# Two attention layers on one core: keys projected from split operands and copied straight into the key stacks, and a new order inside every attention step

## What is computed

```python
x       (16, 100, 256)      # tokens, normalised ahead of each part
ctx     (16, 361, 256)      # context rows, the same for both layers
q = split_heads(queries @ Wq + bq)
k = split_heads(keys @ Wk + bk)
v = split_heads(values @ Wv + bv)
scores = einsum('bhqd,bhkd->bhqk', q, k) / sqrt(HD)
scores = where(mask, -1e15, scores)          # layer 0 only
attn = softmax(scores, axis=-1)
ctx = einsum('bhqk,bhkd->bhqd', attn, v)
out = ctx @ Wo + bo
x = x + tanh(g) * out
```

## Time and profile before

| | us |
|---|---|
| median of three runs | 870.8 (870.23 to 872.3) |
| span of the profiled execution | 871.8 |
| what lies around that span | under 1: the three runs lie between 1.6 below and 0.5 above it |
| attention steps 1 to 14 of layer 0 (73.7 to 317.7) | 244.0 |
| attention steps 1 to 14 of layer 1 (509.7 to 747.2) | 237.5 |
| TensorE busy | 781.5 (90%) |
| VectorE busy | 580.9 (67%) |
| ScalarE busy | 472.6 (54%) |
| mean granted clock of TensorE | 0.965 |

### The profile page before, as it was taken

How to read it: one execution, slowest core, us unless ns; L and a number is a source line. 1 busy time by engine, 2 the same in 40 slices (tenths; PEclk the granted TensorE clock), 3 DMA queues, 4 the chain that set the end, 5 groups by cost and what they waited for, 6 DMA issues and landing times.

```text
span 871.8 us, 22331 instructions
## 1 busy us (share of the span) xinstructions
PE 781.5 (90%) x7992; PEld 603.7 (69%) x7992; DVE 580.9 (67%) x1773; ACT 472.6 (54%) x1012; POOL 213.6 (24%) x212
## 2 busy tenths in 40 slices
PE   5879999999999888999996599999999989888996
PEld 2546777777777665689974476766776667577996
DVE  3777777777787767764545777778788667564333
ACT  2445566566555556356652355655566555654553
POOL 2553132133222406500035522422221111000000
PEclk9899999999999999899998799999999999899999
DMA  7598788868876905623327958798689887000001
GB/s 200 141 225 201 152 157 174 159 147 175 171 166 139 214 17 147 178 93 121 123 77 165 186 128 152 148 190 178 134 182 186 165 170 159 10 1 1 20 19 38
DMA packets 153755, 117.87 MB, mean 135 GB/s; under 512 B 81564, under 2 KB 145160, under 8 KB 153640
## 3 DMA queue, kind: packets, MB, share of 16 engines
q1 hardware_dynamic: 146400, 107.93, 57.5%
q0 software_dynamic: 4096, 6.57, 3.1%
q10 hardware_dynamic: 3152, 1.96, 0.8%
HBM read 76.17 MB, written 38.30 MB: 131 GB/s over the span
## 4 chain that ended last, share of the span: by engine, by line
PE 56%; DMA 15%; SPq 11%; DVE 7%; ACT 5%; issue 4%; ACTq 1%; POOL 0%; DVEq 0%
PE ps L1963 18%; PE ps L2081 7%; DMA cT<-in_ctxT 6%; PE ps L2107 5%; PE ps L2130 4%; PE ps L2140 4%; DMA scr_q<-qp 4%; SPq L477 3%; DMA QS<-mp 3%; PE ps L2126 2%; PE ps L2401 2%; PE ps L2164 2%; SPq L426 2%; DMA QS<-scr_q 2%; SPq L413 2%
## 5 line engine op out<-in xcount | busy, mean ns | idle before, releaser
L1018 ACT ACTIVATE prob<-ps 128x400 f32<-128x400 f32 (+1 forms) x384 | 182.7, 500 | 95.4 <-PE ps L2130 88.8
L2107 PE MATMUL ps<-KS,QS 96*100 96x361 bf16 x512 | 166.9, 342 | 18.1 <-DMA QS<-scr_q 6.2
L1576 DVE CUSTOM_DVE_ANT_0 ps<-ps,biasq 100x361 f32<-100x361 f32 x256 | 135.3, 543 | 54.1 <-PE ps L2107 50.7
L1580 DVE TENSOR_REDUCE mx<-ps 100x1 f32<-100x361 f32 x256 | 127.0, 527 | 57.8 <-PE ps L2107 56.7
L2130 PEld LDWEIGHTS ps<-QS,KS 98*128 98x128 bf16 x1536 | 110.5, 101 | 53.0 <-issue 9.8
L2130 PE MATMUL ps<-QS,KS 98*128 98x100 bf16 x1536 | 135.2, 212 | 8.7 <-ACT prob L1018 4.4
L2081 PE MATMUL ps<-cT,wk 128*128 128x361 f32 x256 | 98.6, 496 | 17.5 <-DMA cT<-in_ctxT 9.9
L2107 PEld LDWEIGHTS ps<-KS,QS 96*100 96x100 bf16 x512 | 64.3, 127 | 54.9 <-DVE mx L1580 14.1
L728 POOL TENSOR_TENSOR kp<-kr,kp 128x722 bf16<-128x722 f32 x32 | 48.7, 1523 | 193.0 <-ACT kp L989 192.7
L2140 PE MATMUL ps<-prob,V 128*17 128x100 f32 (+1 forms) x3072 | 79.8, 252 | 0.2 <-ACT xT L909 0.2
L2140 PEld LDWEIGHTS ps<-prob,V 128*17 128x17 f32 (+1 forms) x3072 | 64.4, 98 | 11.9 <-issue 8.7
(11 more groups left out here) (225 smaller groups left out, 1609.3 us busy)
## 6 DMA issues: line engine op xcount, KB each, us to landing
scr_k<-kp SPq DMA_DIRECT2D x93, 180.5 KB, 5.2
KS<-scr_k SPq DMA_DIRECT2D x62, 270.8 KB, 3.8
cT<-in_ctxT SPq DMA_DIRECT2D x32, 361.0 KB, 5.2
KS<-scr_k SPq DMA_DIRECT2D x62, 180.5 KB, 4.1
QS<-scr_q SPq DMA_DIRECT2D x60, 150.0 KB, 4.2
KS<-scr_k SPq DMA_DIRECT2D x62, 90.2 KB, 4.4
scr_q<-qp SPq DMA_DIRECT2D x42, 100.0 KB, 6.0
xg<-scr_x SPq DMA_DIRECT2D x32, 128.0 KB
```

Of the source, the lines that this page charges most:

```text
L1018: nc.scalar.activation(prob[0:KROWS[t], t, hg, :], ps[0:KROWS[t], c % 2, 0:HQ * S], ACT.Exp).then_inc(a["exp"], 1)
L1576: nc.vector.tensor_tensor_reduce(ps[0:S, banks[h % len(banks)], 0:S2], ps[0:S, banks[h % len(banks)], 0:S2], biasq[p][:, :], 1.0, -3.0e38, ...
L1580: nc.vector.reduce_max(mx[:, h:h + 1], ps[0:S, banks[h % len(banks)], 0:S2], axis=AX.X).then_inc(a["max"], 1)
L2107: mm(ps[0:S, banks[h % len(banks)], 0:S2], QS[p][0:SROWS, h, :], KS[p][0:SROWS, h * S2:(h + 1) * S2], start=True, stop=True).then_inc(a["s ...
```

## The change

Keys are projected from the same halves as values: `wkh`, `wkl` with `cTh`, `cTl`, six fp32r products of 362 columns for each 128 outputs instead of two fp32 matmuls of 361. The weight's low half is made once for each layer. They are projected for batch b + 2 in pairs of products strewn between the first six groups of `score_T`. The DRAM staging is gone: each part is copied from `kp` straight into `KS`, six DMAs for each half, 16 rows of 8 x 361 each. All values of batch b + 2 are projected in the same step, in five pieces between the last scores. `weigh` of quarter 1 moves forward, and `turn_max` stands between `weigh` 2 and `weigh` 3. VectorE's small jobs get fixed places between the maxima. SyncE no longer waits for `QS<-mp` to land; in layer 1 `q_store` moves behind the second half. The two layers share one tile for each attention weight.

The core of the diff:

```diff
+            def k_copy(l, n, half):
                 a, d, p = sa[l], sd, n % 2
-                if half == 0:
-                    sp.wait_ge(d["kst"][p], keys_stored(l, n))
-                    sp.sem_inc(s_held, 1)
                 if n > 1:
                     sp.wait_ge(a["sT"], START + NKT * NHG * (n - 2) + NKT * NHG // 2 * (half + 1))
                     sp.sem_inc(s_held, 1)
                 c = slice(half * HH * S2, (half + 1) * HH * S2)
-                for j, parts in KRUNS:
-                    sp.dma_start(KS[p][j * HD:(j + parts) * HD, c],
-                                 scr_k[p, half, 0:parts].rearrange("j (d h) n -> (j d) (h n)", h=HH)).then_inc(d["kload"][half][p], 16)
+                for part in range(NPIECE):
...
+                    for r in range(NST):
+                        if KPART[r] == part:
+                            sp.dma_start(KS[p][r * HD:(r + 1) * HD, c], kp[:, part, half, :]).then_inc(d["stack"][half][p], 16)
...
+            def project_k(l, n, p, m, products=range(KT * NPIECE)):
+                a = sa[l]
+                if 0 in products:
+                    pe.wait_ge(sc_lo, ctx_parts(l, n))
+                    pe.wait_ge(sw_lo, START + KT * (l + 1))
+                    if n > 0:
+                        pe.wait_ge(a["v_copied"], START + 2 * (n - 1) + m + 1)
+                cols = slice(m * P, (m + 1) * P)
+                for j in products:
+                    k, (wp, xp) = j // NPIECE, ((0, 0), (0, 1), (1, 0))[j % NPIECE]
+                    x = mm(ps[:, key_bank(l, n, m), 0:S2 + 1], (wkh, wkl)[wp][:, k, cols], (cTh, cTl)[xp][p][:, k, 0:S2 + 1],
+                           start=j == 0, stop=j == KT * NPIECE - 1)
...
+                score_T(l, b, u, 2, 2)
...
+                next_score(12)
+                values(1, range(3))
                 score_T(l, b, u, 3, 0)
+                next_score(13)
+                values(1, range(3, 6))
+                score_T(l, b, u, 3, 1)
+                next_score(14)
+                values(2, range(3))
+                score_T(l, b, u, 3, 2)
                 next_score(15)
...
+                weigh(l, b, u, 2)
+                if has_b:
+                    turn_max(l, b + 1, b, 7)
+                weigh(l, b, u, 3)
+                values(2, range(3, 6))
```

VectorE's list in a step, with the number of elements left out:

```diff
-            def step(l, b, u, i, has_o, has_k, has_2, has_b):
+            def step(l, b, u):
...
-                if has_b:
-                    split_max(l, b + 1)
-                if has_k:
-                    k_rest(l, b + 3, 0)
-                if has_2:
-                    ctx_low(l, b + 2, u)
-                if has_k:
-                    k_rest(l, b + 3, 1)
-                if has_o:
-                    stats(2 * l + 1, b - 1, sa[l]["x"], b)
...
+                    if has_2 and i == 4:
+                        k_rest(l, b + 2, 0)
...
+                    if has_2 and i == 9:
+                        k_rest(l, b + 2, 1)
+                    if has_b and i == H - AHEAD - 1:
+                        split_max(l, b + 1)
+                    if b + 3 < B and i == 12:
+                        ctx_low(l, b + 3, 1 - u)
+                    if has_o and i == 13:
+                        stats(2 * l + 1, b - 1, sa[l]["x"], b)
+                    if l == 0 and u == 0 and b >= 2 and i == 14:
+                        stats_end(F0, b - 2, b)
+                    if l == 1 and b + 6 < B and i == 14:
+                        combine(b + 6)
```

652 lines of the change are left out of this document (310 added, 342 removed).

## The result

The changed kernel takes 953.1 us (median of 4 runs, 946.6 to 954.5), the kernel before 870.5 on the same chip. The ratio is 1.092, with an interval of 1.087 to 1.097: slower by 9%. The prediction had the sign right and the size wrong: 912, with a range to 934.

What follows compares the result with a forecast made beforehand. TensorE's list was taken to bound layer 0's steps, with 20.1 us of waits in layer 1. Layer 0 +20.5 and layer 1 +21 made +41.5 on 871.8: 913.3, or 912 as a median, range 885 to 934.

Steps and rivals of the forecast that it cites:

- Keys by parts, -2 us a layer: TensorE's key projection: twelve fp32r products instead of eight fp32 passes, -0.1 us a step, -2 us in each layer.
- The stall at `turn_max`: TensorE waits for VectorE's jobs moved ahead of the maxima's split: +9 us in layer 0, +31 in layer 1.
- The maxima's round trip: A step's first group waits for the maxima's DMA, 0.9 us each: +13.5 us in layer 0, +8 in layer 1.
- What goes away in layer 1, -20: TensorE's waits in layer 1, for context, maxima and exponentials, all vanish: -20 us, only 7 of them sure.
- Outside the steps, 0 give or take 4: Before each layer's first step and in the feed-forward part, less projection and more DMA issue: 0 us, give or take 4.
- The range: Forecast time 885 to 934 us; its low end took layer 0 stalls of 0.4 and 0.7 us as +9.
- The step that failed: SyncE's copies of the stack's second half land 9.6 us behind `turn_max`, head 8 asks after about 10: no cost.
- the straight copy is the late one: Rival: late copies into the stack make head 8 wait 1 us or more in 28 steps, 940 us; chance 0.07.
- The clock: Rival: new waits in layer 1 drop TensorE's clock in ten steps, 2 us each, giving 932 us; chance 0.07.
- Its signs: Expected in the changed profile: waits at `turn_max` and for `QS<-mp`, none for `cT`, steps of 18.5 to 19 us.
- the sign that would prove me wrong: On TensorE, scores waiting for the second half of the stack would refute the forecast; no size given.

Runs made afterwards that it cites:

- e3: Kernel before, with only VectorE's order taken from the change: context low half, statistics, combine and pair statistics ahead of the maxima's split; ratio 1.058.
- e19: Repeat of e5 on e18's chip: changed kernel with VectorE's earlier order and half of the copies left out; ratio 1.015.
- e6: e1 with layer 1's context load issued ahead of the six stores of the queries' pieces instead of behind them; ratio 1.046.
- e1: Changed kernel with VectorE's context low half, statistics and combine back behind the split of the maxima, as before the change; ratio 1.087, median 934.0 us.
- e18: Changed kernel, VectorE's order as changed, with the last three of six copies of each half left out from batch 2 on, keys partly stale; ratio 1.064.
- e5: e1 with the last three of six copies of each half left out from batch 2 on, keys partly stale; ratio 1.011.
- e2: Changed kernel with ten useless matmuls on TensorE ahead of its wait for the split maxima in layer 1; ratio 1.107.
- e13: e8 with three of each half's six copies issued by ScalarE's queue in layer 1, nothing left out; ratio 1.032, median 890.1 us.
- e9: e1 with all six copies of a half issued, but three cut to 16 x 16 elements from batch 2 on; ratio 1.046.
- e8: e6 plus value products moved from the last score stages to around the maxima's transpose, and weight loads issued behind the stack's halves; ratio 1.029.
- e20: e13 with ScalarE issuing three of each six copies in layer 0 too, and the store of query group 3 later; ratio 1.030.

## Why the prediction was wrong in size

**The sum, term by term.** I had +41.5 us, 45.5 of waits in the steps less 4 for the keys. Measured are +20.6 us of waits in layer 0 against +22.5, and +20.9 in layer 1 against +23. That agreement is partly luck, as the terms show, and it is not the whole difference: +26.4 us more is TensorE's busy time, grown where the clock was lower, and +11.1 lies outside the steps.

- *Keys by parts, -2 us a layer.* Right within its size. In nine steps at full clock the busy time is the same to 0.03 us, where I had -0.9.
- *The stall at `turn_max`.* Right in place, and right in price in layer 0: 0.7 to 0.9 us in the steady steps, 11.1 in all for +9. In layer 1 a third too high, 20.4 in all for +31: I had 2.7 a step, and it is 1.8 to 2.3 in eight of steps 1 to 9 and 0.7 or less in the others. e3 has 13.8 and 26.8, together 40.6 for my 40, by luck: there other jobs stand behind other products.
- *The maxima's round trip.* Half as large as said. 0.5 us in a steady step of layer 0 for 0.9, 7.8 in all for +13.5 (2.3 of them in step 1); 1.8 in layer 1 for +8. At the full clock of e19 it is 3.8 in the nine steps that I had counted, 0.4 each; in the changed kernel, by my reading, the half clock stretches the work that covers it.
- *What goes away in layer 1, -20.* The key products' waits for the context did go, 7.4 us. But the context's lateness moved to ScalarE, and with it came 10.0 us of waits for exponentials; for them I had +4 (0 to 12). e6 shows that this one place in the queue holds 21 us once the stall is gone.
- *Outside the steps, 0 give or take 4.* Wrong at the start, +8.7 (3 to 9 in the variants); the +2.5 between the layers are within the scatter of e1 and e6. "More is issued (twelve copies for six loads and three stores)" was in the text, and not what is queued behind them: the store of group 1, for which ScalarE waits 6.25 us.
- *The range.* Its low end is added up wrongly: stalls of 0.4 us in 13 steps and 0.7 in 15, less 2 for the keys, are +13.7 in layer 0 and not +9.

**The step that failed** is the one on SyncE: "I cost that at nothing, with less than a microsecond of cover." I summed 9.6 us from `turn_max` to the landing of the second half, against 10 until head 8 asks. In e1 it is 11.25, and head 8 asks after 9.3: issues of 0.66 for 0.60, and 5.8 us from issue to landing where I took 0.6 and 4.1 from the copies of the start. Halving the copies in the changed kernel itself (e18), with the stalls left in, brings its median from 953.1 to 928.2 and the ratio from 1.092 to 1.064; in the model they were free. The same queue makes the start, steps 1 to 3 and step 14 of layer 0 late; halving the copies (e5) takes 9.5 us from e1's layer 0. I had this as the rival "the straight copy is the late one", 940 with 0.07, and priced it as added to the stalls. In steps 1 to 7 of layer 1 it isn't added: it runs beside them. In layer 0 it is.

**The clock.** I had it at 0.07 and 932, ten steps at 2 us. In the changed kernel the granted clock fell within 1.5 us behind each of the eight stalls of 1.8 to 2.3 us in layer 1, and its busy time grew by 16.7 us there, and by 9.7 in layer 0's disturbed steps. The prediction should have said that stall and clock come together: e3 shows it in the kernel before too, 0.93 for 0.97. In the changed kernel it was no price of its own, though: e2 got the clock back and not the time. The Trainium skill (TensorE: Matmul & The Clock Gate, Why this matters for your kernels) warns of idle gaps between bursts of matmuls. The trace agrees with the warning (a mean clock of 0.84 and 0.91 in turn from step 2 to 6 of layer 1, 1.00 in the same steps of e19), and 0.07 was too little for it.

**Its signs.** `turn_max` waits 2 to 3 us in layer 1 up to step 9 and under 1 in layer 0: seen, but for 1.5 in step 3. About 1 us for `QS<-mp` nearly every step: half of that. No wait of key products for `cT`: seen. Steps of 18.5 to 19 in both layers: 18.3 in layer 0, 20.2 in steps 1 to 7 of layer 1. Shorter steps from 10 on: 16.7 in step 11 and 16.8 in 14, but 20 to 20.6 in 10, 12 and 13, which wait for exponentials and for the queries' load. And I had named the sign that would prove me wrong, scores that wait for the second half of the stack: they do, 5.6 us in layer 0 and 7.2 in layer 1, nearly all of it in steps 12 to 14; before that the stalls hide it.

**What stays open.** e13 brings layer 1 back to 256.7; 5.7 us at the start and 8.9 in layer 0 stay. In layer 0 some 3 us are step 1, 2 are step 15, and the ten steps between 4 and 13 are still 0.4 us longer each than before; I didn't find which order of TensorE's list would close that. Whether fewer and larger transfers from on-chip memory would take the payload's 29 us away wasn't tried.

## What to carry to other kernels

When a stall is taken out and the time stays, look for a second chain of the same length before giving up the theory: a table of two by two, each suspect out alone and both out, shows in three kernels what no list of waits does. Count a DMA three times, for its issue in the queue, for its landing while the others are under way, and for what is queued behind it; what a copy still reads ties its producer to the landing, and a landing measured at the start of this program was too short for its loop.

## What the runs showed of the hardware

- Six copies of 90 KB from on-chip memory took SyncE 3.8 to 6.3 us to issue, median 3.9 (after); three loads from DRAM that bring the same 541 KB took 1.2 to 2.7 us, median 1.25 (before).
- Half of the copies' payload alone, the issues kept, was worth 29 us in 15 steps of layer 1 (e1 to e9), and brought the median landing of the whole copies there from 4.9 to 3.0 us; the DMA share fell from 0.72 to 0.40.
- With the issues shared between two queues the copies landed later, 5.9 us for 4.8 (e13, e8, medians of layer 1), and the steps were shorter all the same.
- With eight idle stalls of 1.8 to 2.3 us TensorE's mean clock in layer 1 was 0.90; with ten matmuls in each, 0.97 (after, e2).
- A copy issued by ScalarE took 0.55 to 1.2 us of its time, median 0.62 (e13). Where TensorE was busy nearly all the time, six of them a step made `xT` late (e20).
